# Where the places of the edge sources are looked up: 49 lookups stay in the init stage, 147 move behind the gathers of the first recurrent step

## The reference

```
h = relu(layernorm(x))
for 5 steps:
    messages = h[col] @ W_msg.T + b_msg        # (row, col) = edge_index = (src, dst)
    agg      = segment_sum(messages, row)
    gi = agg @ W_ih.T + b_ih ;  gh = h @ W_hh.T + b_hh
    r = sigmoid(i_r + h_r) ; z = sigmoid(i_z + h_z) ; n = tanh(i_n + r * h_n)
    h = (1 - z) * n + z * h
x = x + h
```

## Time and profile before

| | us |
|---|---|
| median of 3 runs without the profiler | 5516.6 |
| lowest, highest of them | 5515.52, 5519.96 |
| span of the profiled execution, first to last instruction | 6564.5 |
| init stage in the span: POOL's clearing of `agg` to the first work of the recurrent stage | 3133.78 to 3505.89 |
| step 0 of the recurrent stage: to POOL's first gather of step 1 | 3505.89 to 4096.74 |
| POOL busy, share of the span | 3376.4, 51% |
| PE busy | 4257.9, 65% |
| DVE busy | 3845.9, 59% |

### The profile page before, as it was taken

One profiled execution on the slowest core, in us unless ns is written; L12 is line 12 of the kernel. 1 busy time (PEld: TensorE's weight loads), 2 busy tenths in 40 slices (PEclk: granted clock), 3 DMA queues, 4 the chain that ended last, 5 costly groups with the idle time before them and its releaser, 6 DMA issues. The chain is left out here.

```text
span 6564.5 us, 61506 instructions
## 1 busy us (share of the span) xinstructions
PE 4257.9 (65%) x15022; PEld 2341.7 (36%) x15022; DVE 3845.9 (59%) x7518; ACT 2733.4 (42%) x5325; POOL 3376.4 (51%) x3399
## 2 busy tenths in 40 slices
PE   8944352602344754343577899789889978884586
PEld 5612121300121333232344455455445544442333
DVE  8965530397564255564466676667667756652265
ACT  6822210222222134343476654664465456433432
POOL 8766677046666434544665600640262056556666
PEclk9966676855666877677799999999999999997699
DMA  6722231694111585654476654664465456664444
GB/s 217 256 97 88 80 117 46 238 307 153 40 41 38 195 246 164 179 170 132 140 205 192 213 183 138 201 199 166 150 217 193 138 187 202 214 189 135 123 144 145
DMA packets 628093, 1062.87 MB, mean 162 GB/s; under 512 B 105048, under 2 KB 258158, under 8 KB 627740
## 3 DMA queue, kind: packets, MB, share of 16 engines
q1 hardware_dynamic: 498972, 818.46, 38.6%
q0 software_dynamic: 100544, 163.41, 9.0%
q10 hardware_dynamic: 28224, 77.08, 3.0%
HBM read 599.34 MB, written 464.81 MB: 162 GB/s over the span
## 5 line engine op out<-in xcount | busy, mean ns | idle before, releaser
L1864 POOL DMA_INDIRECT r_G<-msg_tab,srow x784 | 739.6, 943 | 1324.9 <-DMA msg_tab<-r_m 895.0
L860 PE MATMUL l_ps<-cv_V,cv_cwi 128*128 128x448 f32 x896 | 478.3, 702 | 916.7 <-ACT cv_ob L784 457.4
L1254 POOL DMA_INDIRECT x_tab<-a_r,node_pos x392 | 379.6, 968 | 514.7 <-DVE a_r L1211 246.7
L860 PEld LDWEIGHTS l_ps<-cv_V,cv_cwi 128*128 128x128 f32 x896 | 220.4, 253 | 1174.7 <-issue 1161.6
L2113 DVE TENSOR_TENSOR agg<-r_psS,agg 128x128 f32 x980 | 281.7, 287 | 514.7 <-DMA st_o<-o_tab 324.7
L729 POOL DMA_INDIRECT o_tab<-cv_ob,put_idx x392 | 387.7, 989 | 271.9 <-ACT cv_ob L784 147.8
L1945 PE MATMUL r_psR<-r_hin,whh 128*128 128x512 f32 x882 | 463.5, 608 | 27.3 <-ACT r_r L2066 11.4
L1896 PEld LDWEIGHTS r_psM<-wmsg,r_hnew 128*128 128x128 f32 x2744 | 355.8, 195 | 339.5 <-DVE r_hnew L2177 219.1
L1896 PE MATMUL r_psM<-wmsg,r_hnew 128*128 128x128 f32 x2744 | 384.0, 284 | 133.4 <-DVE r_hnew L2177 126.2
L721 POOL DMA_INDIRECT cv_M<-h_tab,gat_src x392 | 373.9, 954 | 119.5 <-issue 119.5
L1181 PE MATMUL l_ps<-a_bmsg,row 128*128 128x512 f32 x196 | 152.5, 871 | 429.3 <-ACT cv_M L1137 271.6
(11 more groups left out here) (292 smaller groups left out, 11307.7 us busy)
## 6 DMA issues: line engine op xcount, KB each, us to landing
r_hin<-ht_tab SPq DMA_DIRECT2D x441, 256.0 KB
msg_tab<-r_m SPq DMA_DIRECT2D x392, 256.0 KB
ht_tab<-r_hnew SPq DMA_DIRECT2D x343, 256.0 KB
o_tab<-o_blank SPq DMA_DIRECT2D x98, 512.0 KB, 6.0
st_h<-h_tab SPq DMA_DIRECT2D x98, 512.0 KB
st_o<-o_tab SPq DMA_DIRECT2D x98, 512.0 KB
r_oin<-ht_tab SPq DMA_DIRECT2D x161, 256.0 KB
i_x<-x_tab SPq DMA_DIRECT2D x49, 528.0 KB
```

The source lines that it names most:

```text
L860: ins = nc.tensor.matmul(psO[:, h, 0:HW], cwi[m][:], V[i % 2][m][:, HW * h:HW * (h + 1)], start=m == 0, stop=m == 3)
L1254: pool.indirect_dma_start(x2_tab, bass.IndirectOffsetOnAxis(ap=node_pos[:, j:j + 1], axis=0), rb[i % RR][:, t, :], None).then_inc(s_out[i ...
L1864: pool.indirect_dma_start(G[g % GR][:, q, :], None, msg_tab[s % 3] if s else first_tab, bass.IndirectOffsetOnAxis(ap=at, axis=0)).then_inc ...
```

## The change

`found` becomes a tensor that outlives the init stage. In init POOL issues one lookup an iteration (columns 0 to 48) in place of four, and DVE's wait and its conversion at the stage's end are gone; POOL waits at its own end for its 49 lookups. In the recurrent stage POOL issues the other 147 lookups (columns 49 to 195) behind the last gather of step 0, then waits until DVE has made `srow`, then goes on to the old wait for the stored messages. DVE makes `srow` in the last part of step 0's second half: between `update(k - 1)` and `hidden(k)` of the job i = 45. Its two scratch rows are now parts of `r_dist`, so ACT waits for `srow` before its first selection of step 1.

```diff
@@ init, POOL
                 for i in range(HALF):
-                    for j in range(TPC * i, TPC * (i + 1)):
-                        pool.indirect_dma_start(found[:, j, :], None, node_tab,
-                                                bass.IndirectOffsetOnAxis(ap=sorted_[:, j, 0:1], axis=0)
-                                                ).then_inc(s_found, 16)
+                    pool.indirect_dma_start(found[:, i, :], None, node_tab,
+                                            bass.IndirectOffsetOnAxis(ap=sorted_[:, i, 0:1], axis=0)
+                                            ).then_inc(s_found, 16)
                     pool.wait_ge(s_xin[i % XR], 16 * (i // XR + 1))
                     nc.gpsimd.tensor_copy(ids[:, :, i, :], xb[i % XR][:, :, :, D].bitcast(I32)).then_inc(s_id, 1)
+                pool.wait_ge(s_found, 16 * HALF)
@@ init, DVE
-                dve.wait_ge(s_found, 16 * EC)
-                do(nc.vector.tensor_copy(srow[:], found[:, :, 1]))
-                table_rows(nc, st, srow[:], row_p[:], row_t[:])
@@ recurrent stage, POOL
                 for s in range(STEPS):
+                    if s == 1:
+                        for j in range(HALF, EC):
+                            pool.indirect_dma_start(found[:, j, :], None, node_tab,
+                                                    bass.IndirectOffsetOnAxis(ap=sorted_[:, j, 0:1], axis=0)
+                                                    ).then_inc(s_found, 16)
+                        pool.wait_ge(s_srow, 1)
                     if s:
@@ recurrent stage, ACT
+                        if s == 1 and i == 0:
+                            act.wait_ge(s_srow, 1)
                         select(HALF * s + i)
@@ recurrent stage, DVE
+                def source_rows():
+
+                    st = Steps(dve, s_dv)
+                    scratch = dist[:].rearrange("p q w -> p (q w)").bitcast(I32)
+                    dve.wait_ge(s_found, 16 * (EC - HALF))
+                    st.mark(nc.vector.tensor_copy(srow[:], found[:, :, 1]))
+                    st.wait()
+                    table_rows(nc, st, srow[:], scratch[:, 0:EC], scratch[:, EC:2 * EC])
+                    dve.sem_inc(s_srow, 1)
...
+                        if s == 0 and i == HALF - 4:
+                            source_rows()
                         hidden(k)
```

More of the change, by code:

```diff
@@ L1369, in build @@
         ids = sb("ids", [P, 2, HALF, TPC], I32, ctx)
+        found = sb("found", [P, EC, 2], I32, ctx)
         x2v = x2_tab.rearrange("(c p t) w -> c p t w", p=P, t=TPC)
@@ L1403, in build @@
             rankf = sb("i_rank", [P, EC], F32, c5)
-            found = sb("i_found", [P, EC, 2], I32, c5)
-            row_p = sb("i_row_p", [P, EC], I32, c5)
-            row_t = sb("i_row_t", [P, EC], I32, c5)
             psT = [pb(f"i_psT{i}", [P, TPC, P], F32, c5) for i in range(2)]
@@ L1698, in build @@
         s_op, s_oe = stage_sem("r_op"), stage_sem("r_oe")
+        s_found = stage_sem("r_found")
+        s_dv, s_srow = stage_sem("r_dve"), stage_sem("r_rows_of_sources")
         c6 = ExitStack()
```

## The result

| | runs | median, us | lowest to highest |
|---|---|---|---|
| kernel before | 12 | 5514.39 | 5501.88 to 5519.96 |
| changed kernel | 12 | 5504.2 | 5494.14 to 5511.98 |

The ratio is 0.9984, 95% interval 0.9977 to 0.9992: 10.2 us gained, where 13 were forecast and 5504 was named. The profiled execution of the changed kernel took 5494.14 us, with a span of 5492.4 us.

A forecast was written before the change was run, and what follows sets the result against it. In the profile init was paced by PE, ACT and DVE plus transfers, never POOL, and step 0's second half by PE. Terms -10 - 4 + 0 + 0 + 1 = -13 us took 5516.6 to 5503.6, rounded to 5504; range 5484 to 5520.

The forecast's parts named there:

- the likeliest case: whole program: 13 us gained, between 8 and 22, with chance 0.45.
- Term 1: init: POOL loses 147 lookups and its lateness of 14.0 us without the profiler; 10 us gained, bounds 0 and 14.
- Term 2: init: 147 lookups' share of the DMA engines goes; 4 us gained, bounds 0 and 7.
- Terms 3 and 4: conversion leaves init's end, hidden by the last store; 147 lookups fit behind step 0's gathers; 0 each.
- the cover: second half of step 0: POOL's idle 297.81 us takes the moved lookups, 101 us to spare.
- Term 5: step 0, job i = 45: conversion adds 1.7 us of DVE between `update` and `hidden`; 1 us lost.
- second rival: init: lookups hold back the whole pipeline, pace falls from 6.38 towards 5.16; -30 us, about 5486; chance 0.10.
- The slower rival: step 0's second half: lookups delay DVE, from 0.37 us each; 20 us longer, 5524; slower ones together 0.10.

The follow-up runs named there:

- the first profile: kernel before, unchanged, profiled ahead of the prediction: span 6564.5 us against a median of 5516.6 us.
- the ordinary profile: kernel before, unchanged, profiled a second time: span 5522.2 us; timed 5512.98 us, ratio 0.9994.
- the run meant to tell: changed kernel plus three clearings of a spare tile ahead of each copy in init: 6541.97 us, ratio 1.0179.
- the third set: runs where the kernel before takes a median of 6417.37 us (6348 to 6566).
- the kernel with slices: changed kernel with `agg` cleared in 49 slices, one behind each POOL copy in init, not in one piece: 6539.4 us, ratio 1.0098.

## Why the prediction was right, and where it was not

- **The total, right, in part by luck.** 10.2 us measured of 13 forecast; the likeliest case came. The items below say what was luck: the first term had a false premise and another path, and the second is not measured by itself.
- **What bounds init, wrong as read.** "POOL therefore never set the pace; it ran ahead and waited" was true of the profiled execution and false of an ordinary one. The prediction did suppose that the timed runs differ there, and only so did it reach the first term, but for the wrong reason: profiled executions take what the others take (5524.01 us beside 5507.62 to 5521.98). Nor does the excess of the first profile lie only ahead of the recurrent stage: of the 1042 us between the two profiles, 610 are ahead of init, 51 in init, 54 in step 0 and 327 behind it. A quarter of a per cent in a program was argued from a profile 19% longer than the runs beside it.
- **Term 1, POOL's path, 10 us: size right, place wrong.** It had POOL late at the end of the stage, with the conversion behind it. In the ordinary profile the last lookup starts at 2826.88 and the last copy at 2828.13, 13 us ahead of the last store at 2841.15:

```profile
2828.13 0.20 POOL L1462 COPY ids<-i_x 128x8 int32<-128x8 int32 x1
2844.31 0.53 POOL L1852 MEMSET r_zero<- 128x512 f32 x1 [15.99 <-POOLq L102]
```

POOL gates through the four load buffers instead: a load waits for the copy out of its buffer, 13 times, 19.7 us. It is the same surplus of POOL's work, paid along the way. That it came near 10 us is in part luck. By the prediction's own path, with the numbers of the ordinary profile, POOL's last copy is 304.8 us into the stage and init ends 5.3 us later (2 + 1.7 + 1.6), at 310.1: 6 us behind the changed kernel's 303.8 and not 17.
- **Term 2, the transfers' share, 4 us: not shown.** Its bound was 7 us for 147 lookups, in proportion to their number. The wait for the state's store fell by 15.6 us between the two kernels' profiles (35.1 to 19.5; another profile with one lookup has 28.8). But moving 98 more lookups, from three to one an iteration, gains nothing clear of the noise (0.9984 both), and the last 49 gain more than the bound (0.9984 to 0.9962, some 12 us; init 303.8 to 314.4 with them, 296.7 and 296.0 without). Neither step is in proportion. How much of the 14 us in init is one term or the other isn't settled; the run meant to tell was spoiled.
- **Terms 3 and 4, the conversion leaving init and the lookups beside the second half, 0 each: right where 5515 us is the time.** 0.9994 for the conversion alone, 0.9998 for the added lookups, 97.65 us to spare of the forecast 101. The lookups took 1.325 us and not 1.245, which the cover absorbs. The prediction's reading of "SBUF — State Buffer" of the Trainium skill ("Who interferes with whom"), that away from init's tensor_scalar they cost what the gathers cost, came out in part: their median is 945 ns like the gathers' 944, but the mean is 994 and the spacing 1.325 us, still near the 1.341 of the earlier trace rows.
- **Term 5, the late conversion, 1 us: nearer 0.** Step 0 took 537.5 and 536.9 us with it, beside 537.1. The operation `r_t` of the job came 1.3 us late once and the next job made it up (below, 3324.80 to 3329.53: 4.73 us and not 6.05). DVE's timeline in the changed kernel:

```profile
3317.44 0.75 DVE L2164 SCALAR_TENSOR_TENSOR r_t<-r_psHN,bhh,r_r 128x512 f32<-128x512 f32 x1 [0.54 <-ACT r_r L2089]
...
3322.86 0.26 DVE L2118 COPY srow<-found 128x196 int32<-128x196 int32 x1
...
3324.80 0.75 DVE L2164 SCALAR_TENSOR_TENSOR r_t<-r_psHN,bhh,r_r 128x512 f32<-128x512 f32 x1 [0.24 <-DVE srow L75]
...
3329.53 0.75 DVE L2164 SCALAR_TENSOR_TENSOR r_t<-r_psHN,bhh,r_r 128x512 f32<-128x512 f32 x1 [0.18 <-ACT r_r L2089]
```

- **"The first term cannot be seen in a profile", wrong.** An ordinary profile shows it plainly, and the pace did fall by 0.40 us, which the prediction had listed as near its second rival. That rival had the lookups hold the whole pipeline back by their transfers and named 5486; with no lookup at all in init the kernel came to 5495.21, so something of it may be real, though no run isolates it.
- **The slower rival, the lookups hold up the second half: false where 5515 us is the time, true in its outcome in the third set**, and by waits of 20 to 58 us on PE, ACT and DVE, not by the 0.37 us for each lookup that was put on DVE.

Moving all 196 is the best version measured (5495.21 us), and on the third chip the same kernel is 2.2% slower than before. The change itself was not timed there; the kernel with slices, which moves the same 147 lookups, was 1.0% slower. Neither it nor the slices of `agg` can be recommended unseen: no kernel with slices was timed where the kernel before takes 5515 us.

## What to carry to other kernels

Hold a profile's span against the timed runs before reading a single stage; where they differ by 19%, who bounds a stage may differ too, and a second profile of the same kernel costs one run. A helper engine that is done before the stage ends can still gate it, through the buffers it must release: compare its work per iteration (5.78 us) with the pace (5.90), and ask how long its own waits are (0.2 us is none). Small transfers issued back to back in an engine's idle half cost nothing on two chips and 180 to 250 us of that stage on a third, so such a move is timed on more than one chip.

## What the runs showed of the hardware

- The pace of init by lookups an iteration: none 5.35 (5.34 and 5.36 in the third set), one 5.49, 5.56 and 5.73 (5.40 in the third set, with slices), three 5.61, four 5.90, 5.88 and 5.98, five 6.97 us. It rises by some 0.1 us a lookup up to three, by 0.3 for the fourth and by 1.1 for the fifth, as POOL's own work (5.78 us with four) passes the pace of the rest.
- One clearing of `agg` on POOL stretched a cast of DVE from 0.34 to 15.2 us, to the clearing's own end (14.1 to 15.5 us in all twelve runs that clear it in one piece). "SBUF — State Buffer" of the Trainium skill ("Who interferes with whom") says that casts can take the port pair shared with GpSimd, and that the second to come is blocked for the whole instruction; these rows agree to 0.1 us.
- The same kernel before takes 5517 and 5518 us on two chips and 6417 on a third, and moving all 196 lookups gains 0.4% on one of the first and loses 2.2% on the third.
